# Tridiagonal reduction of a 128 x 128 matrix inside a graph network kernel: the next row summed in PSUM from three products, and the block's sweeps spread over ten steps

## The reference

```python
h = relu(layernorm(x)); x = x + L0(h, adj, W1, b1, W2, b2)        # spectral
h = relu(layernorm(x)); x = x + L1(...)                           # two-layer network with batch norms
h = relu(layernorm(x)); x = x + L2(...)                           # two graph convolutions, then LSTMs over windows of 1 to 4 rows
h = relu(layernorm(x)); x = x + L3(...)                           # attention with a mask
# L0:
L_norm = d_inv_sqrt[:, None] * (diag(deg) - A) * d_inv_sqrt[None, :]
_, U = eigh(L_norm)                                               # all eigenvectors of a symmetric 128 x 128 matrix
out = relu(einsum('mn,bnd->bmd', U.T, h) @ W1 + b1) @ W2 + b2
return einsum('nm,bmd->bnd', U, out)
```

## Time and profile before

| what | us |
|---|---|
| median of 3 runs | 1569.76 |
| the profiled execution, its own time | 1570.16 |
| its span, first to last instruction | 1568.5 |
| tridiagonal form, ends at 411.1 | 390 |
| search pass 0, first to last iteration | 53.0 |
| search pass 1, first to last iteration | 45.8 |
| twisted factorization | 71 |

### The profile page before, as it was taken

The page is one execution under the profiler, slowest core; times in us unless marked ns, Lnnn a source line. Parts: engine busy times, 40 slices in busy tenths (PEclk is TensorE's granted clock), DMA queues, the critical chain, the costliest instruction groups (busy, mean ns, idle before and its releaser), DMA issues.

```text
span 1568.5 us, 21564 instructions
## 1 busy us (share of the span) xinstructions
PE 1124.1 (72%) x5260; PEld 714.5 (46%) x5260; DVE 1045.5 (67%) x4156; ACT 690.6 (44%) x1760; POOL 253.9 (16%) x900
## 2 busy tenths in 40 slices
PE   3777777776542300448787668999999998589998
PEld 2445555555421200335453356444455443367777
DVE  7777788777889999755576754444343354664766
ACT  2334444444231200024365457675554545365665
POOL 4045555666450000000000000000010020000000
PEclk9999999999975555559898679999999999597999
DMA  4000000000100000000000000000000000000001
GB/s 138 1 1 1 1 1 1 1 1 2 29 21 1 1 0 0 1 0 0 0 0 0 0 0 0 0 0 0 0 0 0 0 0 0 0 15 13 27 20 34
DMA packets 16654, 12.30 MB, mean 8 GB/s; under 512 B 665, under 2 KB 14530, under 8 KB 16578
## 3 DMA queue, kind: packets, MB, share of 16 engines
q1 hardware_dynamic: 16578, 11.49, 2.6%
HBM read 7.23 MB, written 4.19 MB: 7 GB/s over the span
## 4 chain that ended last, share of the span: by engine, by line
PE 50%; DVE 35%; issue 7%; ACT 4%; DVEq 1%; DMA 1%; POOL 1%; ACTq 0%; POOLq 0%
PE P L1343 30%; PE P L690 9%; PE P L1492 4%; DVE B L348 2%; DVE arena L330 2%; DVE arena L444 2%; DVE arena L495 1%; DVE arena L493 1%; DVE scal L320 1%; DVE bst_all L909 1%; ACT hb L1154 1%; DVE arena L448 1%; DVE arena L259 1%; DVE arena L337 1%; PE P L1485 1%
## 5 line engine op out<-in xcount | busy, mean ns | idle before, releaser
L1343 PE MATMUL P<-arena,WT 128*128 (+2 forms) x792 | 329.1, 579 | 3.9 <-ACT L1242 2.9
L1343 PEld LDWEIGHTS P<-arena,WT 128*128 128x128 f32 x792 | 151.8, 192 | 181.1 <-issue 167.3
L690 PE MATMUL P<-arena 1*128 1x127 f32 (+62 forms) x504 | 166.1, 434 | 87.1 <-DVE arena L330 48.6
L1255 ACT ACTIVATE arena<-P,bl 128x512 f32<-128x512 f32 (+1 forms) x252 | 153.3, 636 | 139.5 <-PE P L1343 130.7
L690 PEld LDWEIGHTS P<-arena 1*128 1x128 f32 x504 | 124.1, 307 | 142.4 <-DVE arena L330 112.8
L898 POOL COPY arena<-arena 128x512 f32<-128x512 f32 x16 | 21.5, 1386 | 783.0 <-DVE arena L1075 691.2
L1064 DVE TENSOR_TENSOR arena<-arena 128x512 f32<-128x512 f32 (+1 forms) x36 | 22.0, 610 | 137.4 <-ACT arena L1255 137.4
L652 ACT ACTIVATE arena<-arena 1x127 f32<-1x127 f32 (+62 forms) x126 | 32.2, 256 | 167.5 <-DVE arena L341 157.2
L1154 ACT ACTIVATE hb<-xN,nmr,rsd 128x128 f32 (+1 forms) x192 | 78.5, 481 | 34.9 <-PE P L1343 28.1
L690 PE MATMUL P<-arena,Ib 128*128 128x46 bf16 (+1 forms) x318 | 34.4, 268 | 60.9 <-ACT arena L679 60.4
L195 POOL TENSOR_SCALAR lf<-lf 1x1 f32<-1x1 f32 x210 | 73.3, 349 | 21.9
(11 more groups left out here) (477 smaller groups left out, 2451.2 us busy)
## 6 DMA issues: line engine op xcount, KB each, us to landing
out_dram<-xN SPq DMA_DIRECT2D x16, 256.0 KB, 2.3
Wn<-in_L_gnn_Wih_dram SPq DMA_DIRECT2D x4, 256.0 KB, 2.9
Wn<-in_L_gnn_Whh_dram SPq DMA_DIRECT2D x4, 256.0 KB, 2.8
Wqkv<-in_L_gnn_W_dram SPq DMA_DIRECT2D x1, 192.0 KB, 3.6
W1n<-in_L_gnn_W_dram SPq DMA_DIRECT2D x1, 128.0 KB, 4.1
W2n<-in_L_gnn_W_dram SPq DMA_DIRECT2D x1, 128.0 KB, 4.0
Wg<-in_L_gnn_Wg_dram SPq DMA_DIRECT2D x2, 64.0 KB, 3.6
adj<-in_adj_dram SPq DMA_DIRECT2D x1, 64.0 KB, 1.8
```

What stands on the lines that cost most here:

```text
L690: def mm(o,l,r,start=True,stop=True): return t.matmul(o,lhsT=l,rhs=r,start=start,stop=stop)
L1255: act(s.gt[u][gate][:,0:cols],P[4*u+gate][:,0:cols],f,bias=s.bl[:,4*(p-1)+gate:4*(p-1)+gate+1]).then_inc(ev('lstm_gates'),1)
L1343: def mm(o,l,r,start=True,stop=True,**k): return t.matmul(o,lhsT=l,rhs=r,start=start,stop=stop,**k)
```

## The change

It has three parts.

*Row b.* The product `P<-B,I` no longer reads the updated `B`. Row k+1 is summed in P0 over three products that are issued at three places: from the old `B` as soon as ScalarE has copied the last row b out of P0; `Bv` times `v` between the two outer products; and `v` times `w` right behind the reflector's column. `P<-B,xcol` is then the only product of a step that waits for the update. Each of the two new products is one number times a row.

*Spots.* A sweep has 20 spots, ten steps, and the pieces stand at phases 0, 2, 6, 7 and 10. Eleven sweeps lie in the tridiagonal form; the other five go on through all of pass 0, all of pass 1, and the first 53 iterations of the twisted factorization. ScalarE's root of sweep 11 now stands ahead of the fifth sign operation of pass 0.

*More on GpSimd.* VectorE keeps what is a scan, a reduction or a reciprocal: 6 operations per sweep, where it had 13. The other seven go to GpSimd (`gamma`, the new diagonal and its products, the pick, the radicand, the shift), which gets one or two more where it has no fused form.

```diff
-SPOTS=16
+SPOTS=20
@@ GpSimd
-        def new_offdiagonals(sweep):
-            eng.wait_ge(ev('leaf_from_vector'),5*sweep)
-            l(tt(rows(300,20),rows(200,20),rows(240,20),ALU.mult))
-            l(tt(rows(300,20),rows(300,20),rows(142,100),ALU.mult))
-            l(tt(leaf_4e2,row(300,15),row(320,15),ALU.mult))
-            l(ts(leaf_n4,leaf_4e2,-1.0,None,ALU.mult))
+        def new_block(sweep):
+            eng.wait_ge(ev('leaf_from_vector'),5*sweep+1)
+            l(tt(leaf_gamma[:,0:16],leaf_q,leaf_rz,ALU.mult))
+            l.mark(tt(rows(300,20),rows(200,20),rows(240,20),ALU.mult))
+            l.mark(tt(leaf_sums16,leaf_gamma[:,0:16],leaf_gamma[:,1:17],ALU.subtract))
+            l.wait(l.n-1)
+            ...                      # six more, two chains in turn
+            l(ts(leaf_dd,leaf_d[:,0:15],4*EPS*EPS,None,ALU.mult))
+            l(tt(leaf_dd,leaf_dd,leaf_d[:,1:16],ALU.mult))
@@ VectorE, leaf_at
             if phase==2 and sweep:
                 v.wait_ge(ev('leaf_from_gpsimd'),5*sweep)
                 c(v.tensor_tensor_scan(leaf_z[:,1:16],leaf_t,ones[0:1,0:15],1.0,ALU.mult,ALU.add))
-                c(v.reciprocal(leaf_rz,leaf_z[:,0:16]))
-                tt(leaf_gamma[:,0:16],leaf_q,leaf_rz,ALU.mult).then_inc(ev('leaf_from_vector'),1)
-            if phase==3 and sweep:
-                ...                  # three operations
-            if phase==5:
+                v.reciprocal(leaf_rz,leaf_z[:,0:16]).then_inc(ev('leaf_from_vector'),1)
+            if phase==6:
                 v.wait_ge(ev('leaf_from_gpsimd'),5*sweep+1)
-                c(v.tensor_reduce(leaf_idx,leaf_hot,AX.X,ALU.max))
-                ts(leaf_pick,...).then_inc(ev('leaf_from_vector'),1)
+                v.tensor_reduce(leaf_idx,leaf_hot,AX.X,ALU.max).then_inc(ev('leaf_from_vector'),1)
             ...                      # phases 6 and 8 become 7 and 10, with one operation each
@@ search and twisted factorization
-                if pass_==0 and i%2 and HH_SPOTS+i//2<=SPOTS*(SWEEPS-1)+8: leaf_at(HH_SPOTS+i//2)
+                if i%2: leaf_at(HH_SPOTS+HN//2*pass_+i//2)
+            if i%2 and HH_SPOTS+HN+i//2<=SPOTS*(SWEEPS-1)+10: leaf_at(HH_SPOTS+HN+i//2)
@@ TensorE, hh_step(k)
             mm(P[4][:,0:1],reflector(k),I[0:1,0:1]).then_inc(ev('column_psum'),1)
+            if k: mm(P[0][0:1,k:N],v_row[:,k+1:k+2],w_row[:,k:N],start=False).then_inc(ev('row_b_psum'),1)
             t.wait_ge(ev('B_updated'),k+1)
-            mm(P[0][0:1,k:N],I[:,k+1:k+2],B[:,k:N]).then_inc(ev('row_b_psum'),1)
+            if not k: mm(P[0][0:1,0:N],I[:,1:2],B[:,:]).then_inc(ev('row_b_psum'),1)
             t.wait_ge(ev('column'),k+1)
             mm(P[1][0:1,k:N],xcol[:,:],B[:,k:N]).then_inc(ev('row_xB'),1)
+            t.wait_ge(ev('row_b'),k+1)
+            if k+1<K: mm(P[0][0:1,k+1:N],I[:,k+2:k+3],B[:,k+1:N],stop=False)
             t.wait_ge(ev('Bv'),k+1)
             t.wait_ge(ev('v_scaled'),k+1)
             mm(P[3][:,k+1:N],Bv_row[:,:],v_row[:,k+1:N],stop=False)
+            if k+1<K: mm(P[0][0:1,k+1:N],Bv_row[:,k+2:k+3],v_row[:,k+1:N],start=False,stop=False)
             t.wait_ge(ev('w_row'),k+1)
             mm(P[3][:,k+1:N],v_row[:,:],w_row[:,k+1:N],start=False).then_inc(ev('outer_products'),1)
```

More of the change, by code:

```diff
@@ L202, in rotations @@
             tt(leaf_t,leaf_t,leaf_4e2,ALU.mult).then_inc(ev('leaf_from_gpsimd'),1)
-        def new_offdiagonals(sweep):
-            eng.wait_ge(ev('leaf_from_vector'),5*sweep)
-            l(tt(rows(300,20),rows(200,20),rows(240,20),ALU.mult))
-            l(tt(rows(300,20),rows(300,20),rows(142,100),ALU.mult))
-            l(tt(leaf_4e2,row(300,15),row(320,15),ALU.mult))
-            l(ts(leaf_n4,leaf_4e2,-1.0,None,ALU.mult))
+        def new_block(sweep):
[4 more added lines that the diff above has]
+            l.wait(l.n-1)
+            l.mark(tt(rows(300,20),rows(300,20),rows(142,100),ALU.mult))
+            l.wait(l.n-1)
+            l.mark(ts(leaf_sums16,leaf_sums16,0.5,None,ALU.mult))
+            l.wait(l.n-1)
+            l.mark(tt(leaf_4e2,row(300,15),row(320,15),ALU.mult))
+            l.wait(l.n-1)
+            l.mark(tt(leaf_d[:,0:16],leaf_sums16,leaf_d[:,1:17],ALU.add))
+            l.wait(l.n-1)
+            l.mark(ts(leaf_n4,leaf_4e2,-1.0,None,ALU.mult))
+            l.wait(l.n-1)
+            l(ts(leaf_dd,leaf_d[:,0:15],4*EPS*EPS,None,ALU.mult))
+            l(tt(leaf_dd,leaf_dd,leaf_d[:,1:16],ALU.mult))
         def alive(sweep):
-            if sweep: eng.wait_ge(ev('leaf_from_vector'),5*sweep+1)
             l.mark(tt(leaf_diffs[:,0,:],leaf_n4,leaf_dd,ALU.add))
@@ L246, in _ @@
                 rotations(sweep)
-                new_offdiagonals(sweep)
+                new_block(sweep)
             alive(sweep)
@@ L663, in _ @@
             sweep,phase=divmod(2*(k-LEAF_FROM),SPOTS)
-            if sweep>=0 and phase==6: leaf_root_of(sweep)
+            if sweep>=0 and phase==8: leaf_root_of(sweep)
         net.scalar_pre(a)
@@ L675, in _ @@
             for sweep in range(SWEEPS):
-                i=2*(SPOTS*sweep+6-HH_SPOTS)+1
-                if h<HALVES and i>0 and i//(SEG//2)==h: leaf_root_of(sweep)
+                root_spot=SPOTS*sweep+8-HH_SPOTS
+                if root_spot>=0 and root_spot//(SEG//4)==h: leaf_root_of(sweep)
             a.wait_ge(ev('sturm_half'),h+1)
@@ L681, in _ @@
             if h%HALVES==HALVES-1: shared_signs(h)
+        for sweep in range(SWEEPS):
+            if SPOTS*sweep+8-HH_SPOTS>=HN: leaf_root_of(sweep)
         a.wait_ge(ev('norm2'),1)
```

24 lines of the change are left out of this document (10 added, 14 removed).

## The result

The changed kernel takes 1574.5 us (median of 9 runs, 1573.4 to 1582.7) against 1568.95 us (9 runs, 1567.7 to 1571.3) on the same chip: the ratio is 1.0049, 95% interval 1.0034 to 1.0064. It is slower by 5.6 us, where 15.4 us of gain were forecast. Its runs fall in two groups, six near 1573.9 us and three near 1582.5; the profiled one took 1582.5 us, so from the traces about 9 us more are to be explained than from the medians.

The account below looks back on a forecast made before the run. TensorE was taken to bound wide steps, VectorE's row of scalars narrow ones. Gains of 9.5 (row b) and 12.2 (block) less losses of 1, 1.6, 2 and 1.7 gave 15.4 us, so 1554 us, range 1546 to 1563.

Parts of the forecast that it names:

- Row b, the price: TensorE's small added products, mainly the one between the outer products, were to lose 1 us.
- its own sign: Narrow steps: the prediction is wrong if the outer products move apart by more than 0.05 us.
- Another of its signs: Early form: the prediction is wrong if row b's 9.5 us don't appear in the first 50 steps.
- rival A: TensorE's new products hold the second outer product back at full length, 24 us; about 1572 us; 4 in 100.
- Row b, the gain: Wide steps: the product with the column starts earlier, 0.31 us at 123 columns, nil at 59; 9.5 us gained.
- The block in the tridiagonal form: Eleven sweeps with fewer VectorE operations were to cost 2.8 us instead of 15; 12.2 us gained.
- Phase 2: Block sweep in the form, keeping a scan and a reciprocal: some 0.3 us over a free step.
- Phase 6: Block sweep in the form, a single VectorE operation: was to cost next to nothing.
- GpSimd: In the form, its 10.05 us piece fits into five steps, 12.4 us; VectorE was not to wait for it.
- Pass 0: First search pass: VectorE waits 5.9 us in place of 2.3; 1.6 us lost.
- Pass 1: Second search pass, clean before, gets one and a half sweeps and GpSimd's company: 2 us lost, 1 to 3.
- The twisted factorization: Stage behind the passes: nine operations cost 0.9 us, waits 0 to 1.4; 1.7 us lost, 0.8 to 3.

Follow-up runs that it names:

- e1: The changed kernel with TensorE's product order of before and no small products, so only the block's part is left: 1552.3 us, ratio 0.9898.
- e4: The changed kernel with both small products left out (results not the reference's), P<-B,I behind the product with the column: 1556.9 us, ratio 0.9905.
- e5: The changed kernel with the product with the column waiting for the column's copy first, the update of B second: 1573.1 us, ratio 1.0021.
- e11: e4 with the wait swap of e5, so no small products and results not the reference's: 1540.9 us, ratio 0.9819.
- e7: e1 plus one product of one data column between the outer products, into a bank nobody reads: 1568.3 us (one run).
- e2: The kernel before with TensorE's new order alone (row b summed from three products), the block as it was: 1586.0 us, ratio 1.0113.
- e9: e5 with the first outer product's two waits also swapped, from 91 columns down: 1569.4 us, ratio 0.9996.
- e6: e1 with VectorE's two waits swapped in front of Bv and of the update of B: 1540.2 us, ratio 0.9797.
- e10: e6 with waits also swapped before v.Bv, x_next, h and, in narrower steps, the first outer product: 1529.2 us, ratio 0.9737.

## Why the prediction was wrong

**Row b, the price, is the step that failed.** It was put at 1 us; it is 23. Against e1, the time from the start of `w` to the next update, summed over the 125 steps of the changed kernel, is 23.1 us longer; with the small products left out (e4) it is 0.7 shorter. The sum was 0.94 us between the outer products at 123 columns, 0.57 of them for the first, and 0.36 for the new one, which just fits. In the trace after, the first takes 0.71 until the narrow weights can be loaded (42.30 to 43.01) and the new one 0.49 until the next wide ones (43.50): 1.20. Both numbers had been taken from products whose weights have one form, `P<-B,I` and `P<-B,xcol`, or an outer product before another wide one; none of the rows showed a change of form, and this was not bounded. In narrow steps the prediction trusted that "most of the gap is still wait for `w`" and counted 0.03 to 0.05 us; it is 0.27 at 59 columns. No row was read for that gap in a narrow step. It is 0.59 us at 59 columns (e1: 247.09 to 247.68), and 0.57, the prediction's own number for one outer product at 123 columns, leaves next to nothing in it. By its own sign it was wrong there: the outer products were to stay within 0.05 us of where they were, and are 0.85 us apart (257.08 to 257.93), where it was 0.56 before. Another of its signs failed too: at the 50th step the changed kernel is 3.5 us behind, not 9.5 ahead.

The price can also be read without the gain in it. e5 and e11 have their waits in the same order, and e11 has no small product: 422.6 against 389.2, 33.4 us. So 10.9 us could be had (e11 against e1), 33.4 are paid, and e5 stands 22.5 behind e1.

This is rival A, in place and in total, and in part by luck. It named the second outer product that is held back, and 24 us for it. But it took the price to be the columns alone, 0.36 us at 123 and 0.17 at 59; measured from `w` to the update it is 0.26 and 0.22, and e7 shows that some 10 us of it do not depend on the columns. (Two passes of `P<-B,I` at 59 columns take 0.22 us in the trace before, 252.72 to 252.94, and not 0.17.) Its total of 1572 came near 1574.5, though it assumed row b's full 9.5 us.

**Row b, the gain: the size was right, but it was not reached.** What was to be had is 10.9 us (e11) against 9.5. In e4, 8.4 of them are gone to one wait: two semaphores in front of a product become a separate instruction and a wait on the load, and the copy of the column, which ends last, got the separate one. That costs 0.09 us in each step in which the copy decides. The prediction took its 0.05 us behind the later of update and copy from a product that waited for one semaphore. Before, `P<-B,I` carried the wait for the update, so each product with `B` had one. The trace before has the other case, at the first outer product, whose second wait (706) is for the scaled `v`: at 58 columns its weights start 0.12 us behind that copy (253.76 to 253.88).

```profile
L706 PEldq EVENT_SEMAPHORE  x126: 51/51/51, 23.5 to 409.7; - x126
```

In the changed kernel this wait is there as well, but it decides nothing: without it the last update comes 0.1 us earlier (e5), since narrow steps wait for the outer products. What holds wide steps back is the product `v.w`, counted at nothing: at 123 columns the product with the column starts 0.22 us behind the copy (41.02 to 41.24), and 0.10 in e11 (39.22 to 39.32). The time from the update to `Bv`, summed over all steps, is 3.5 us longer in e5 than in e11.

**The block in the tridiagonal form: 10.8 us instead of 12.2 by itself (e1), right;** beside row b's part it is 6.2 (e2). Phase 2 costs 0.23 us (e1: 3.02 us at 60 columns, 2.79 beside it), forecast 0.3 over a free step; in steps of over 70 columns it costs nothing. Phase 6 was to be free, and is not in every sweep:

```profile
249.25 0.15 DVE L340 TENSOR_TENSOR arena<-arena,scal 1x1 f32<-1x1 f32 x1
249.53 0.15 DVE L385 TENSOR_REDUCE lf<-lf 1x1 f32<-1x15 f32 x1
249.64 0.26 DVE L344 SCALAR_TENSOR_TENSOR arena<-arena,scal,P 1x59 f32<-1x59 f32 x1
```

In this step of e1 the sum over 15 columns starts 0.28 us behind 340 and `Bv` 0.11 behind it, and the step takes 3.04 us. One sweep later, at 49 columns, the sum starts 0.08 us behind 340 (277.65 and 277.73), and nothing is lost. About half of the eleven steps with phase 6 lose 0.1 to 0.25 us. The piece has a wait for GpSimd in front of it, which phase 0's reciprocal has too; why it starts late in some steps is open.

**GpSimd** made VectorE wait nowhere in the form, as forecast. **Pass 0** costs 1.0 us more (54.0 against 53.0) for 1.6 forecast, with a wait of 6.4 for 5.9. **Pass 1** takes 47.4 us, 1.6 more, for 2. **The twisted factorization** takes 71.5 us, 0.9 more, for 1.7. Together 3.5 for 5.3, the direction right in each.

**What is left** is TensorE's clock late in the program. At the end of the twisted factorization the changed kernel is 15.5 us behind, e1 7.7 ahead; at the end e1 is 18.9 us ahead in its profiled run. The windows 1400 to 1460 us, before and then e1 (columns: window, length, busy us and count of each engine, granted clock as a share, DMA share, GB/s):

```profile
1400.00:1460.00 60.00, 57.99 (x430) 45.64 (x430) 33.30 (x65) 34.39 (x67) 0.00 (x0) 0.83 0.06 18
```

```profile
1400.00:1460.00 60.00, 57.76 (x525) 46.34 (x525) 42.59 (x82) 41.74 (x81) 0.00 (x0) 1.00 0.07 22
```

At a mean of 0.83, a third of the 60 us is at 1.2 GHz instead of 2.4. It lies in two spells of some 10 us (1411 to 1421 and 1438 to 1448), through which TensorE is busy, as it was before them. If the work of such a spell goes at half speed, the two cost 10 us, by estimate. The changed kernel's profiled run has two spells as well, one in these 60 us (mean 0.91) and one from 1519 to 1529. e5, which differs by one swap of waits and 0.1 us in the last update, was profiled in a run of 1573.6 us, and has neither. At the end of the twisted factorization it is 0.7 us ahead of the changed kernel, at the end of the program 9.0. Changed kernel, then e5:

```profile
1510.00:1530.00 20.00, 19.48 (x124) 15.10 (x123) 8.88 (x18) 10.96 (x22) 0.00 (x0) 0.74 0.04 13
```

```profile
1510.00:1530.00 20.00, 19.15 (x183) 15.46 (x177) 14.63 (x28) 13.10 (x25) 0.00 (x0) 1.00 0.09 26
```

So the 9 us between the changed kernel's two groups are probably these spells, and the 5.6 us between the medians are about the 15.5 less a pair of them, which the kernel before has in its profile. What sets them off is open. It is not the program alone: beside e5 and beside e9 the kernel before ran 17 times each, and 3 and 2 of these took about 1583 us where the others took 1569, with a mean clock of 0.87 against 0.88; none of the five was profiled. Of e1's 16.4 us some 8 belong to its work, and the rest seems to be this.

The Trainium skill, "Perfetto Trace Analysis", section "Identifying Dependency Chains", says that an instruction that waits for several engines may get semaphore instructions put in front of it. The trace agrees and adds the price, 0.09 us on TensorE and 0.07 on VectorE (e5, e6). The Trainium skill, "TensorE: Matmul & The Clock Gate", section "Step-by-step: what each phase is for", says that the weights of a later product are pulled ahead of products under way if they go to the background buffer or to other rows. Here the load of wide weights behind wide ones starts 0.12 us behind the start of the pass before it (e1: 247.94 to 248.06), well before that pass is over, but the load of narrow ones behind wide ones only after 0.34 us (e7).

## What to carry to other kernels

A small product slipped between two others costs far more than its columns: measure the time from pass to load across the change of weights, and don't take it from products of one form. If an instruction waits for two semaphores, see in the trace which wait stands apart, and order them so that the one that ends last is on the instruction itself; in a chain of 126 short steps this alone was worth 21 us (e1 to e10). When a wait is taken out of a step and the step stays as long (e5), look for the parallel chain that had been as late.

## What the hardware showed that was not expected

- Weights of one row and one column behind weights of 128 columns: 0.34 us from the start of the last pass to the next pass, 0.29 at 10 columns of data, against 0.21 from wide to wide. Back to wide ones it is 0.12 us from the narrow load at one column of data (e7), 0.28 at 59, 0.49 at 122 (changed kernel).
- Of two waits, the one written last is separate. It costs 0.09 us until a product starts on TensorE (0.07 until its weights do) and 0.07 us on VectorE, but only if it ends last.
- TensorE, busy all the while, fell to half clock for spells of some 10 us, about 5 us of time each by estimate. Two kernels that differ by the order of two waits had two spells in one profile and none in the other (changed kernel, e5).
